# Router weights as eight more columns of the last gate slice, and the slices in the order third, first, second

## The reference, cut to what matters

```
logits = x @ gate_w.T                       # x: 4096 x 512, gate_w: 8 x 512
probs = softmax(logits); top 2 of 8 experts, their weights divided by their sum
shared = silu(x @ sw_gate) * (x @ sw_up) @ sw_down    # 512 -> 352 -> 512
out = routed + shared                       # routed: the two chosen experts of each token
```

## Time and profile before

| what | us |
|---|---|
| median of 3 runs | 2401.06 (2394.18 to 2403.63) |
| profiled execution, its own time | 2400.2 |
| its span, first to last instruction | 2398.5 |
| PE busy in the span | 2204.7 (92%) |
| DVE busy | 1481.4 (62%) |
| POOL busy | 1155.1 (48%) |
| ACT busy | 1026.3 (43%) |
| shared stage in the trace, about | 1469 to 1842 |

### The profile page before, as it was taken

One profiled execution on the slowest core, in us unless ns is written; L12 is line 12 of the kernel. 1 busy time (PEld: TensorE's weight loads), 2 busy tenths in 40 slices (PEclk: granted clock), 3 DMA queues, 4 the chain that ended last, 5 costly groups with the idle time before them and its releaser, 6 DMA issues. The chain is left out here.

```text
span 2398.5 us, 32362 instructions
## 1 busy us (share of the span) xinstructions
PE 2204.7 (92%) x11791; PEld 1383.0 (58%) x11791; DVE 1481.4 (62%) x3297; ACT 1026.3 (43%) x1925; POOL 1155.1 (48%) x730
## 2 busy tenths in 40 slices
PE   6999399999999999999999996999996999999998
PEld 5777244444444444444444433777774878778787
DVE  4665487776777777677776734565554565555554
ACT  3333045556555555555555563312222343333432
POOL 0000035566475665655566575445554344444443
PEclk9999589999999999999999998899998999999999
DMA  5765810402313132151402101434324666566662
GB/s 163 259 248 213 183 36 19 102 23 54 89 36 89 32 79 51 44 139 37 101 24 54 56 25 55 139 106 152 112 89 161 194 194 209 184 208 205 193 207 83
DMA packets 168255, 278.68 MB, mean 116 GB/s; under 512 B 28571, under 2 KB 71067, under 8 KB 168096
## 3 DMA queue, kind: packets, MB, share of 16 engines
q1 hardware_dynamic: 145152, 210.43, 30.1%
q0 software_dynamic: 22944, 66.19, 8.7%
HBM read 191.25 MB, written 88.71 MB: 117 GB/s over the span
## 5 line engine op out<-in xcount | busy, mean ns | idle before, releaser
L887 ACT ACTIVATE b_pt<-b_st 128x512 f32<-128x512 f32 (+3 forms) x1280 | 612.3, 535 | 486.3 <-DVE b_st L849 206.6
L704 POOL TENSOR_TENSOR b_acc<-b_acc,b_pt 128x1024 f32<-128x1024 f32 (+1 forms) x256 | 592.7, 2347 | 214.1 <-ACT b_pt L887 213.9
L828 DVE TENSOR_REDUCE b_mpart<-b_mx 128x1 f32<-128x512 f32 x768 | 511.7, 685 | 197.2 <-PE b_mx L944 194.4
L965 PE MATMUL b_st<-b_q,b_k 97*128 97x512 f32 (+2 forms) x1280 | 495.1, 400 | 75.4 <-ACT b_pt L887 54.6
L944 PE MATMUL b_mx<-b_k,b_q 96*128 96x512 f32 (+2 forms) x1280 | 506.9, 411 | 26.9 <-DVE b_mt L836 23.0
L944 PEld LDWEIGHTS b_mx<-b_k,b_q 96*128 96x128 f32 x1280 | 247.0, 194 | 282.0 <-DVE b_mpart L828 154.0
L965 PEld LDWEIGHTS b_st<-b_q,b_k 97*128 97x128 f32 x1280 | 241.1, 190 | 280.4 <-ACT b_pt L887 240.4
L978 PE MATMUL b_ob<-b_pt,b_v 128*32 128x512 f32 (+3 forms) x2560 | 302.9, 545 | 1.1 <-ACT b_pt L887 1.1
L825 DVE CUSTOM_DVE_ANT_0 b_unread<-b_mx,b_later 128x384 bf16<-128x384 f32 (+3 forms) x512 | 244.5, 484 | 87.7 <-PE b_mx L944 87.2
L704 POOL TENSOR_TENSOR b_acc<-b_pt 128x1024 f32<-128x1024 f32 x48 | 113.3, 2378 | 296.3 <-ACT b_pt L887 296.3
L76 PE MATMUL e_fb<-e_xh,e_w_guh 128*128 128x512 f32 (+3 forms) x552 | 203.3, 368 | 11.5 <-DVE e_w_dl L1827 10.0
(11 more groups left out here) (242 smaller groups left out, 3387.2 us busy)
## 6 DMA issues: line engine op xcount, KB each, us to landing
b_q<-scr_qh SPq DMA_DIRECT2D x64, 256.0 KB, 4.5
b_k<-scr_kh SPq DMA_DIRECT2D x64, 256.0 KB, 4.1
sw_gu<-in_L_ffn_w_gate_dram SPq DMA_DIRECT2D x12, 704.0 KB, 4.4
sw_gu<-in_L_ffn_w_up_dram SPq DMA_DIRECT2D x12, 704.0 KB, 6.1
a_xin<-in_L_attn_x_dram POOLq DMA_DIRECT2D x8, 1024.0 KB, 5.8
scr_qh<-a_qh SPq DMA_DIRECT2D x8, 1024.0 KB, 5.0
scr_ql<-a_ql SPq DMA_DIRECT2D x8, 1024.0 KB, 7.1
scr_kh<-a_kh SPq DMA_DIRECT2D x8, 1024.0 KB, 4.4
```

The costliest lines, as they stand in the source:

```text
L704: g.tensor_tensor(out[:, :, lo:], so_far[:, :, lo:], pt[n % NPB][:, :, lo:], ALU.add).then_inc(s_add, 1)
L828: v.tensor_reduce(part, mxb[i % NMX][:, 0:w], AX.X, ALU.max).then_inc(s_red, 1)
L887: act.activation(pt[n % NPB][:, j, lo:], stb[:, (2 * n + j) % NST, lo:], ACT.Exp, scale=SCALE).then_inc(s_exp, 1)
L965: pe.matmul(stb[:, (2 * n + j) % NST, lo:], kb[:, h, at:at + P], qb[:, h, q * CH + lo:(q + 1) * CH], start=True, stop=True).then_inc(s_st, 1)
```

## The change

The weight tiles `guh` and `gul` of the shared expert get 8 more columns in each row (352 + 8), and the router's weights are put into the 8 that stand behind the gate's third slice. The third slice's gate product then has 96 + 8 = 104 columns of weights, and rows 96 to 103 of its bank are the logits. The product `logits` goes. For that the slices are made in the order third, first, second (`SLICES`), on PE, ACT and DVE. `expert_rows` takes rows 96 to 103 of fb0 to the same rows of `lgT`, and in the usual step it comes ahead of hidden 0. The second use of fb0 also waits for that copy. In the last step PE starts with the gate of the first slice made and turns the logits right behind it. `down` starts with the slices third and first and ends with the second. The setup writes the high and low gate and up weights into rows of 360 instead of 352.

```diff
...
-    def __init__(self, al, name, raw=None):
+    def __init__(self, al, name, raw=None, more=0):
...
-        self.guh, self.gul = al.sb(f"{name}_guh", [P, 2, KD, F], F32R), al.sb(f"{name}_gul", [P, 2, KD, F], F32R)
+        self.guh, self.gul = al.sb(f"{name}_guh", [P, 2, KD, F + more], F32R), al.sb(f"{name}_gul", [P, 2, KD, F + more], F32R)
...
-def gate_up(nc, bank, wt, which, f, xh, xl):
...
-    lo, w = FS[f]
+def gate_up(nc, bank, wt, which, f, xh, xl, more=0):
...
+    lo, w = FS[f][0], FS[f][1] + more
...
-def down(nc, bank, wt, hh, hl, t, slices=range(NF)):
+def down(nc, bank, wt, hh, hl, t, slices=range(NF), order=range(NF)):
...
-                  wt.dh[0:w, f], wt.dl[0:w, f], f == 0, f == NF - 1)
+                  wt.dh[0:w, f], wt.dl[0:w, f], f == order[0], f == order[-1])
...
-        gwh, gwl = al.sb("c_gwh", [P, KD, E], F32R), al.sb("c_gwl", [P, KD, E], F32R)
-        wt = FfnWeights(al, "c_sw", ahead.raw)
+        wt = FfnWeights(al, "c_sw", ahead.raw, E)
+        guh, gul = wt.guh[:, :, :, 0:F], wt.gul[:, :, :, 0:F]
+        gwh, gwl = wt.guh[:, 0, :, F:F + E], wt.gul[:, 0, :, F:F + E]
+        SLICES = (NF - 1,) + tuple(range(NF - 1))
+        LG = FS[NF - 1][1]
...
-        lgT = al.sb("c_lgT", [E, CH])
+        lgT = al.sb("c_lgT", [LG + E, CH])
...
-                def hidden(c, f, first=False):
+                def hidden(c, i, first=False):
+                    f = SLICES[i]
...
-                    act.wait_ge(s_gu, (c * NF + f) * 2 + 2)
+                    act.wait_ge(s_gu, (c * NF + i) * 2 + 2)
...
-                        act.wait_ge(s_h, (c - 1) * NF + f + 1)
-                    act.activation(sg[0:w, f], fb[2 * f % 5][0:w, :], ACT.Silu).then_inc(s_sg, 1)
-                    act.wait_ge(s_h, c * NF + f + 1)
+                        act.wait_ge(s_h, (c - 1) * NF + i + 1)
+                    act.activation(sg[0:w, f], fb[2 * i % 5][0:w, :], ACT.Silu).then_inc(s_sg, 1)
+                    act.wait_ge(s_h, c * NF + i + 1)
...
-                act.activation(gwh[:], gw[:], ACT.Copy).then_inc(s_wh, 1)
-                act.activation(wt.guh[:], wt.gu[:], ACT.Copy).then_inc(s_wh, 1)
+                act.activation(gwh, gw[:], ACT.Copy).then_inc(s_wh, 1)
+                act.activation(guh, wt.gu[:], ACT.Copy).then_inc(s_wh, 1)
...
                 def expert_rows(c):
-                    v.wait_ge(s_lt, c * 2 + 1)
-                    v.tensor_copy(lgT[:], lb[0:E, :]).then_inc(s_ltc, 1)
+                    v.wait_ge(s_gu, c * NF * 2 + 1)
+                    if c:
+                        v.wait_ge(s_lt, c)
+                    v.tensor_copy(lgT[LG:LG + E], fb[0][LG:LG + E, :]).then_inc(s_ltc, 1)
...
                 def token_rows(c, first=False):
-                    v.wait_ge(s_lt, c * 2 + 2)
+                    v.wait_ge(s_lt, c + 1)
...
-                def hidden(c, f, first=False):
+                def hidden(c, i, first=False):
+                    f = SLICES[i]
...
-                    v.wait_ge(s_sg, c * NF + f + 1)
+                    v.wait_ge(s_sg, c * NF + i + 1)
...
-                        v.wait_ge(s_hl, (c - 1) * NF + f + 1)
-                    v.tensor_tensor(hf[0:w, f], sg[0:w, f], fb[(2 * f + 1) % 5][0:w, :], ALU.mult).then_inc(s_h, 1)
-                    v.wait_ge(s_hh, c * NF + f + 1)
+                        v.wait_ge(s_hl, (c - 1) * NF + i + 1)
+                    v.tensor_tensor(hf[0:w, f], sg[0:w, f], fb[(2 * i + 1) % 5][0:w, :], ALU.mult).then_inc(s_h, 1)
+                    v.wait_ge(s_hh, c * NF + i + 1)
...
-                v.tensor_tensor(gwl[:], gw[:], f32(gwh[:]), ALU.subtract).then_inc(s_wl, 1)
-                v.tensor_tensor(wt.gul[:], wt.gu[:], f32(wt.guh[:]), ALU.subtract).then_inc(s_wl, 1)
+                v.tensor_tensor(gwl, gw[:], f32(gwh), ALU.subtract).then_inc(s_wl, 1)
+                v.tensor_tensor(gul, wt.gu[:], f32(guh), ALU.subtract).then_inc(s_wl, 1)
...
                     else:
+                        expert_rows(c)
...
-                        expert_rows(c)
...
-                def logits(c, first=False):
...
-                    if not first:
-                        pe.wait_ge(s_slot, c)
-                    for k in range(KD):
-                        ins = mm3(nc, lb[0:E, :], gwh[:, k], gwl[:, k], xh[:, k], xl[:, k], k == 0, k == KD - 1)
-                    ins.then_inc(s_lt, 1)
...
                 def turn_logits(c):
...
-                        ins = pe.transpose(lb[:, t * E:(t + 1) * E], lgT[:, t * P:(t + 1) * P], ident[0:E, 0:E])
+                        ins = pe.transpose(lb[:, t * E:(t + 1) * E], lgT[LG:LG + E, t * P:(t + 1) * P], ident[LG:LG + E, LG:LG + E])
...
-                def hidden(c, f, first=False, both=range(2)):
+                def hidden(c, i, first=False, both=range(2)):
...
-                        n = 2 * f + which
+                        n = 2 * i + which
...
+                            pe.wait_ge(s_ltc, c * 2 + 1)
...
-                        gate_up(nc, fb[n % 5][:], wt, which, f, xh, xl).then_inc(s_gu, 1)
...
-                def down_rows(c, ts, slices):
-                    pe.wait_ge(s_hl, c * NF + slices[-1] + 1)
+                        gate_up(nc, fb[n % 5][:], wt, which, SLICES[i], xh, xl, 0 if n else E).then_inc(s_gu, 1)
...
+                def down_rows(c, ts, some):
+                    pe.wait_ge(s_hl, c * NF + some[-1] + 1)
+                    slices = [SLICES[i] for i in some]
...
-                        ins = down(nc, fb[(2 * NF + t) % 5][:], wt, hh, hl, t, slices)
-                        if slices[-1] == NF - 1:
+                        ins = down(nc, fb[(2 * NF + t) % 5][:], wt, hh, hl, t, slices, SLICES)
+                        if some[-1] == NF - 1:
...
                     if last:
-                        logits(c)
...
                     else:
...
-                        logits(c, first)
...
```

## The result

| | device us, median (range) | beside the kernel before | ratio, 95% interval |
|---|---|---|---|
| the changed kernel, 5 runs | 2386.69 (2378.54 to 2389.62) | 2403.63 (2394.18 to 2406.02) | 0.993 [0.9906, 0.9954] |
| the same on another chip, 6 runs | 2381.25 (2374.49 to 2387.75) | 2402.55 (2394.56 to 2413.28) | 0.9904 [0.988, 0.9929] |

What follows compares the result with a forecast made beforehand. The prediction took PE to bound the kernel, busy 41.38 of each 41.66 us step. Seven steps' 19.3 us plus the last step's 1.7 made 21.0 us, taking the median from 2401.06 to 2380.0 us, range 2373 to 2390.

Steps and rivals of the forecast that it cites:

- PE sets the pace, and 12 matmuls are 2.76 us a step: Seven usual steps: PE bounds each, and 12 logits matmuls removed at 0.230 us give 2.76 us a step, 19.3 in all.
- Eight more columns cost nothing: Third slice's gate product: 104 columns of weights instead of 96 add 0 us, the longer loads being hidden.
- The copy moved costs nothing; o_low 0.78 us ahead: Usual step on DVE: copying the logits ahead of hidden 0 costs nothing, and o_low ends 0.78 us before att.
- Rival 3: Usual steps: o_low comes late, losing over 0.78 us; a miss of 1 us each gives 2387 us; 7 in 100.
- The last step, 1.7 us: Last step: token_rows, and with it the stage's end, comes 1.70 us sooner; bounds 0 and 2.76.
- Rival 2: Last step: the clock falls after PE's two waits of about 0.9 and 1.0 us; 2380.0 to 2381.6 us; 7 in 100.
- Setup 0: Setup: writing gate and up weights in rows of 360 changes nothing; bounds 1 us up or down.
- Rival 1: Around the logits product: array mode changes go too, 1.6 us more gain over 8 chunks, 2378.4 us; 8 in 100.
- Rival 4: Usual steps: a chain outside PE holds the 41.66 us, so no gain, 2401 us; 4 in 100.
- The sum: Whole kernel: 19.3 us from usual steps and 1.7 from the last give 21.0 us, 0.87% less.

Runs made afterwards that it cites:

- the last experiment: The changed kernel with POOL's multiplication held until c_hl is done and two low splits of the down weights moved behind residual tiles in the setup: 2381.8 us, ratio 0.9899.

## Why the prediction was right, step by step

**PE sets the pace, and 12 matmuls are 2.76 us a step.** Right in kind and nearly in size. Shown from both sides: +12 gives +2.79, -9 gives -2.08, the merged kernel plus the product is back at 41.74. The undisturbed step fell by 2.70, 0.225 a matmul. By the Trainium skill, "TensorE: Matmul & The Clock Gate", section "Back-to-back issue gap", with about 131 ns a matmul, doubling the product would have cost an estimated 12.6 us in 8 chunks; 22.9 were measured, so these runs do not agree with that figure for this stream.

**Eight more columns cost nothing.** Right to 0.07 us a step, which holds the 0.06 that separates 2.70 from 2.76. Rows of 360 without the columns took 41.67, so little or none of it is the row length.

**The copy moved costs nothing; o_low 0.78 us ahead.** Right: 0.90. With the copy left behind hidden 0 it is 0.06, not 0.17, and still no wait. Rival 3 did not come. Its factor of 1.3, and the 1 us that bounded the setup, were a misreading of the earlier trace rows: DVE is not slowed beside POOL, it waits for one POOL instruction and then runs at its pace (see the last section).

**The last step, 1.7 us.** The order of events was right, the size came out smaller. In us from the last step's start:

| | before | after | turn behind the up product |
|---|---|---|---|
| token_rows | 6.09 | 4.31 | 6.19 |
| POOL's first store of entries | 13.56 | 11.76 | 13.64 |
| POOL's first gather for the experts | 31.66 | 30.38 | 31.77 |
| start of PE's last down matmul | 29.63 | 27.91 | 31.53 |
| the experts' first matmul | 42.34 | 41.06 | 44.22 |

The wait for the turn was 0.88 where 0.9 were forecast, and the stores and the down product came 1.80 and 1.72 us sooner, as forecast. The experts' first matmul came only 1.28 sooner. In no profile does it come less than 10.68 us behind the first gather or less than 12.68 behind the last down matmul, and in twelve of fourteen it comes within 0.1 us of the later of these two bounds. Before, both fell together; after the change it is the gather that decides. And from the first store to the first gather, a stretch in which POOL waits for the entries to land, it is 18.0 to 19.0 us (21.0 in the kernel with a quarter of the product): 18.1 before, 18.6 after. So 1.80 us did come off the chain, as the forecast has it, and 0.52 of them went into the spread of this stretch, which the forecast did not allow for; in the other profiles of the merged kernel with PE's order left as it is the last step lasted 40.64 to 41.42, 0.9 to 1.7 less than before. With the turn moved the down product is the later one.

Rival 2, a clock that falls there, did not come: behind the two waits of 0.88 and 0.89 us no gate, up or down matmul of lines 77 and 78 took more than 0.40 us. It came where the turn was moved, behind a wait of 3.84 us, and cost 1.3 us at the stage's end.

**Setup 0.** Right for the layout: the wide low part took 4.24 us against 4.23, and the setup 29.52 with rows of 360 and the product kept. The 0.42 us less (29.09 against 29.51) goes with the clock, whose mean there was 0.77 instead of 0.73; the merged kernel's profile with the turn moved, at 0.73, had 29.48.

**Rival 1, mode changes.** No sign. A matmul is worth 0.231 us where 9 go, 0.232 where 12 come and 0.231 where 12 come on top of the merged kernel; where 12 go and the 8 columns come it is 0.225; a price for passing from wide to narrow weights would be the same at 24, 12 and 3 and gone at 0, and the merged step would have been shorter than 38.90. Rival 4, a chain outside PE that holds the step, fell with the steps of 38.96.

**The sum.** 21.0 forecast, 21.16 in the stage of the profile, but that they agree to 0.2 is luck. Seven steps at 2.70 are 18.9 us (forecast 19.3), the last step 1.3 (1.7) and the setup 0.4 (0): 20.6 in all. Two things that the forecast did not have cancel nearly: 2.7 us come from step 0 being at the high clock from its start, which the forecast took to be at the low one in both kernels, and 2.2 are lost in two steps by DVE behind POOL. In the repeated run they are 2.7 and 1.1. The 7.66 us outside the stage are the spread of unchanged parts: the span up to the first att was 1472 to 1486 us in the profiles of this study, and the experts took either 555.9 to 556.6 us, or 558.6 as in this one, the order-only one and the last.

**What the measurement leaves.** 2386.69 lies 6.7 us above 2380.0. Of that 2.6 is the kernel before, which came at 2403.63 instead of 2401.06; the other 4.1 are within what five executions with a range of 11 us can tell. The second chip gave 2381.25.

## What to carry to other kernels

Where one engine is busy for all but 0.3 us of a step, the distance between starts of the matmuls removed was the gain, and one run with the product doubled tells that before any rewrite. A narrow product that shares its moving data with a wider one cost next to nothing as 8 extra columns beside 96; first look where its result goes, since a chain that leans on it decides the last, uncovered step. Compare such a change stage by stage, cut at instructions that both kernels have: here unchanged parts moved by 8 us in the very execution that was to show 21.

## What was not expected of the hardware

**DVE behind POOL.** A DVE instruction on SBUF tiles that starts 0.02 to 0.17 us behind POOL's `oin` multiplication lasts until that is done and its own work on top (c_hl 4.98 to 5.12 us instead of 0.69; a 128 x 4 copy 4.56). One that starts first, or at the same time, is not delayed, and POOL's multiplication then lasts up to 5.16 us instead of 4.60, the more the longer the two overlap. DVE's `c_xl`, which reads PSUM and SBUF, took 0.68 to 0.69 us in all 136 cases in which it began while POOL's multiplication ran. The profile counts the delay as busy time, not as a wait, so only a duration that is far off its like gives it away. POOL's start hangs on the landing of the `rin` DMA, so it happens by chance: 9 times in the 60 meetings of the ten profiles without a hold, each for 1.1 to 1.3 us of a step. It was 3 of 30 where the logits come from their own product alone, 6 of 30 in the others; whether the change makes it likelier is open.

The setup of every profile has it too, in both directions, and the earlier trace rows shows a part of it. After:

```profile
1481.39 7.93 POOL L1258 TENSOR_TENSOR rin<-c_xin,wo_b 128x512 f32<-128x512 f32 x4 [6.81 <-DVE c_ol L1390]
...
1482.81 1.18 DVE L1489 TENSOR_TENSOR c_sw_gul<-gate_w,c_sw_guh 128x32 fp32r<-128x32 f32 x1 [1.60 <-ACT c_sw_dh L1367]
1483.92 4.24 DVE L1490 TENSOR_TENSOR c_sw_gul<-sw_gu,c_sw_guh 128x2816 fp32r<-128x2816 f32 x1
```

POOL's first three additions take 1.30 to 1.32 us each. DVE's small subtraction begins 0.17 us behind the second and its large one 0.03 behind the third: 1.18 us for 128 x 32, which took 0.26 in the last experiment, where it began near the end of an addition, and 1 us more for 128 x 2816 than the 3.25 of the experts' two halves. POOL's fourth addition begins inside the large one and takes 4.17 us instead of 1.30.

The Trainium skill's "SBUF — State Buffer", section "SBUF: two separate sides", says that DVE and GpSimd share a pair of ports that whichever starts first holds for its whole instruction, for DVE operations with two SBUF inputs or in a 2-port mode; the traces agree with it, in both directions, for these POOL instructions. One case does not fit: DVE's four sums `c_sooner` (128 x 8, both inputs in SBUF) of each last step begin 0.05 to 0.64 us into POOL's `c_ex` (1.04 us, 128 x 4) and take 0.16 us as everywhere else. That stays open.

**The clock in unchanged parts.** In the experts' stage PE waits 1.64 to 1.67 us for the down weights' low part six times, some 70 us apart. Behind two or three of these waits the clock falls for about ten matmuls, behind the others it doesn't, and which ones differs between executions. The first of them, 136 us into the stage, after, then the same place before (a matmul at 0.59 to 0.63 us is one at the lower level, 1.2 GHz; the two windows, from the wait on, have a mean granted clock of 0.57 and 1.00):

```profile
1961.99 0.49 PE L76 MATMUL e_fb<-e_xh,e_w_guh 128*128 128x512 f32 x1 [1.65 <-DVE e_w_dl L1826]
1962.32 0.59 PE L77 MATMUL e_fb<-e_xh,e_w_gul 128*128 128x512 f32 x1
...
1965.27 0.63 PE L78 MATMUL e_fb<-e_xl,e_w_guh 128*128 128x512 f32 x1
...
1977.07 0.50 PE L76 MATMUL e_fb<-e_xh,e_w_guh 128*128 128x512 f32 x1 [1.67 <-DVE e_w_dl L1827]
1977.41 0.40 PE L77 MATMUL e_fb<-e_xh,e_w_gul 128*128 128x512 f32 x1
1977.65 0.39 PE L78 MATMUL e_fb<-e_xl,e_w_guh 128*128 128x512 f32 x1
```

The three profiles with 558.6 us in the experts have three such falls and 36 or 37 matmuls over 0.55 us, the eleven others two falls (the earlier trace rows is one) and 23 to 26. The third fall costs 1.6 us: to the next such wait it is 70.7 us instead of 69.1. The other 1.0 us lies ahead of the first of these waits and was not followed.

In the same way step 0 starts with 12 to 14 low-clock matmuls (2.5 to 2.7 us) in seven profiles and with none in seven. The logits' own product doesn't bring it: the merged kernel with the product had none, and the merged kernels with the turn behind the up product or the shorter setup had them. It goes with when PE, at the low level in the first matmuls of att, comes to the high one: 4.1 to 4.9 us into att in the seven with a slow start of step 0, 3.0 to 3.1 or 5.5 us in the seven without. What decides that stays open. Of the five kernels with unmerged logits all had the slow start, of the nine merged ones two, so the change may have a hand in it; these profiles can't settle that.
